# Local attention on one core: two of sixteen query/key projections of a repeat take another place in the written order

## The reference, cut to what matters

```python
def attn_layer(x, Wqkv, qs, ksc, Wo):          # 16 heads of 64
    q, k, v = split(x @ Wqkv, 3)
    q, k = l2norm(q) * qs, l2norm(k) * ksc
    q = q * cos * scale + rotate_half(q) * sin * scale
    k = k * cos / scale + rotate_half(k) * sin / scale
    out = local_attention(q, k, v)             # windows of 32: own window and the one before, softmax
    return out @ Wo
for i in range(6):
    x = attn_layer(shift_tokens(x), ...) + x
    x = ffn_layer(shift_tokens(x), ...) + x    # layer norm, gated GELU
```

## Time and profile before

| | |
|---|---|
| median of 3 runs | 4428.97 us (4423.1 to 4429.79) |
| profiled execution | 4426.65 us |
| its span, first to last instruction | 4424.9 us |
| mean granted TensorE clock | 0.991 of full speed |
| PE busy | 4276.1 us, 97% |
| DVE, ACT, POOL busy | 74%, 59%, 49% |
| matmul instructions, weight loads | 68360 each |

### The profile page before, as it was taken

The page is one execution under the profiler, slowest core; times in us unless marked ns, Lnnn a source line. Parts: engine busy times, 40 slices in busy tenths (PEclk is TensorE's granted clock), DMA queues, the critical chain, the costliest instruction groups (busy, mean ns, idle before and its releaser), DMA issues.

```text
span 4424.9 us, 159360 instructions
## 1 busy us (share of the span) xinstructions
PE 4276.1 (97%) x68360; PEld 2558.4 (58%) x68360; DVE 3267.2 (74%) x5759; ACT 2617.6 (59%) x5346; POOL 2168.4 (49%) x1986
## 2 busy tenths in 40 slices
PE   8999999999799999999999999999999999999998
PEld 5555555555356656656666656656656656656655
DVE  5666666565577878877887877877877777877875
ACT  5544555455356666666666666666666666666664
POOL 0000000000266766766766766766766766766763
PEclk9999999999899999999999999999999999999998
DMA  1000000000111112111121111211122111221112
GB/s 45 4 8 6 8 6 6 6 8 4 46 47 50 48 46 68 50 50 49 49 69 52 48 46 50 69 49 50 48 60 58 44 51 46 62 60 49 49 47 67
DMA packets 141403, 185.95 MB, mean 42 GB/s; under 512 B 32870, under 2 KB 63652, under 8 KB 140708
## 3 DMA queue, kind: packets, MB, share of 16 engines
q1 hardware_dynamic: 140708, 175.76, 14.6%
HBM read 26.76 MB, written 4.19 MB: 7 GB/s over the span
## 4 chain that ended last, share of the span: by engine, by line
PE 70%; issue 1%; DVE 1%; POOL 1%; DMA 0%; SPq 0%; ACT 0%; DVEq 0%; POOLq 0%; ACTq 0%
PE psum L1599 23%; PE psum L1540 10%; PE psum L1604 8%; PE psum L1616 8%; PE psum L1525 6%; PE psum L1637 6%; PE psum L1609 4%; PE psum L1642 3%; PE psum L1562 1%; PE psum L1622 1%; PE psum L1632 0%; POOL qk L1489 0%; POOL cs L1480 0%; DVE cs L1779 0%; DVE rots L1743 0%
## 5 line engine op out<-in xcount | busy, mean ns | idle before, releaser
L1480 POOL TENSOR_TENSOR cs<-cs 128x512 f32<-128x512 f32 x768 | 975.6, 1276 | 545.2 <-DVE cs L1779 526.6
L1599 PE MATMUL psum<-wqkv,xw 128*128 128x512 f32 x2304 | 1184.1, 613 | 10.1 <-DMA wqkv<-in_wqkv 10.1
L1779 DVE TENSOR_TENSOR cs<-psum,rots 128x1024 f32<-128x1024 f32 x768 | 935.1, 1218 | 244.8 <-PE psum L1599 237.0
L1489 POOL TENSOR_TENSOR qk<-cs,rn 128x512 f32<-128x512 f32 x768 | 776.4, 1042 | 407.9 <-ACT rn L1663 407.9
L1676 ACT ACTIVATE sq<-psum 128x512 f32<-128x512 f32 x768 | 459.6, 598 | 538.7 <-DVE cs L1779 176.1
L1508 POOL MEMSET tiled<- 128x128 bf16 x1 | 0.2, 204 | 1170.0 <-POOLq L590 1170.0
L1736 DVE TENSOR_REDUCE ss<-sq 128x8 f32<-128x512 f32 x768 | 519.7, 677 | 11.7
L1540 PEld LDWEIGHTS psum<-pT,vw 64*64 64x64 f32 x18432 | 401.0, 135 | 203.4 <-issue 203.1
L1599 PEld LDWEIGHTS psum<-wqkv,xw 128*128 128x128 f32 x2304 | 371.0, 191 | 179.7 <-issue 139.9
L1540 PE MATMUL psum<-pT,vw 64*64 64x32 f32 x18432 | 446.5, 222 | 22.8 <-issue 18.0
L1604 PEld LDWEIGHTS psum<-ident,qk 128*128 128x128 f32 x3072 | 352.6, 141 | 168.9 <-issue 158.6
(11 more groups left out here) (198 smaller groups left out, 6639.0 us busy)
## 6 DMA issues: line engine op xcount, KB each, us to landing
vw<-vl SPq DMA_DIRECT2D x768, 128.0 KB, 2.4
vw<-vl SPq DMA_DIRECT2D x672, 64.0 KB, 2.0
wqkv<-in_wqkv SPq DMA_DIRECT2D x36, 256.0 KB, 4.2
wol<-in_wol SPq DMA_DIRECT2D x6, 512.0 KB, 3.8
xin<-in_x SPq DMA_DIRECT2D x9, 256.0 KB, 2.9
xr<-in_x SPq DMA_DIRECT2D x8, 256.0 KB, 3.0
sums<-sumout SPq DMA_DIRECT2D x8, 256.0 KB, 2.3
cs<-sums SPq DMA_DIRECT2D x8, 256.0 KB, 4.6
```

Of the source, the lines that this page charges most:

```text
L1480: summed_rot.done(nc.gpsimd.tensor_tensor(own, own, halves(cs[:, t % 2, j, 1, :])[:, :, ::-1, :], ALU.add), at)
L1489: rotated.done(nc.gpsimd.tensor_tensor(qk[:, j, :].rearrange("p (h c) -> p h c", c=EL), cs[:, t % 2, j, 0, :].rearrange("p (h c) -> p h c" ...
L1599: last = nc.tensor.matmul(ps[:, :], xw[:, t * P:(t + 1) * P], wqkv[:, col:col + BANK], start=True, stop=True)
L1779: parts.done(V.tensor_tensor(cs[:, t % 2, j, :, :].rearrange("p i (h c) -> p i h c", c=EL), twice, by_head, ALU.mult), at)
```

## The change

Two names move in `BODY`, and nothing else is edited.

```diff
--- before.py
+++ after.py
@@ -252,10 +252,10 @@
 BODY = [step(name) for name in """
     qk.0.0 t.3.0 qk.0.1 t.3.1 t.3.2 t.3.3 qk.0.2 qk.0.3 n.0 y2.0 pt.2.0 qk.1.0 sa.3
     v.0.0 pt.2.1 s.3.0 s.3.1 v.0.1 t.0.0 t.0.1 w.3 t.0.2 qk.1.1 t.0.3 oa.2
-    qk.1.2 o.2.0 o.2.1 qk.1.3 pt.3.0 sa.0 n.1 pt.3.1 v.1.0 s.0.0 s.0.1 qk.2.0
+    qk.1.2 o.2.0 o.2.1 qk.1.3 pt.3.0 sa.0 n.1 pt.3.1 v.1.0 qk.2.0 s.0.0 s.0.1
     v.1.1 t.1.0 w.0 t.1.1 oa.3 t.1.2 qk.2.1 o.3.0 o.3.1 t.1.3 qk.2.2 pt.0.0
     qk.2.3 v.2.0 sa.1 pt.0.1 qk.3.0 s.1.0 s.1.1 n.2 w.1 y v.2.1 t.2.0
-    t.2.1 xt oa.0 t.2.2 t.2.3 o.0.0 o.0.1 qk.3.1 pt.1.0 pt.1.1 xn qk.3.2
+    t.2.1 xt oa.0 t.2.2 qk.3.1 t.2.3 o.0.0 o.0.1 pt.1.0 pt.1.1 xn qk.3.2
     qk.3.3 sa.2 v.3.0 v.3.1 s.2.0 s.2.1 n.3 gate.0 gate.1 w.2 up.0 gate.2 oa.1
     up.1 up.2 o.1.0 o.1.1
 """.split()]
```

## The result

The changed kernel takes 4454.76 us (median of four runs, 4452.6 to 4457.89); the kernel before takes 4426.03 on the same chip. The ratio is 1.0065, with a 95% interval of 1.0049 to 1.0081: slower by 28.7 us, 22 to 36 by the interval. The profiled executions have spans of 4450.8 and 4424.9, 25.9 us apart; the granted clock is 0.99 in both. Forecast were 16 us more, between 4425 and 4460. Two later executions, one of b_only and one of v_swap, ran at a granted clock of 0.75 and 0.66 and are left out of every comparison.

The account below looks back on a forecast made before the run. The prediction took PE's order to bound the kernel, with pauses for its own instructions. Gains of 28.5 us against costs of 44.6 gave 16.1 more: 4428.97 + 16 = 4445 us, 4436 to 4457 by the terms (8 in 10: 4425 to 4460).

Parts of the forecast that it names:

- oa.3: First move: this step waits for DVE's first centring, behind the product of `qk.2.0`; 0.50 us a repeat, 23.0 us cost.
- sa.2: Second move: this step waits for ACT's copy of `pt.1.0`, last of four behind a square; 15.6 us cost.
- sa.0: First move: new wait for `o.2.0`'s copy, tie lost by 0.03 us, 0.10 for a further waiting instruction; 6.0 us cost.
- o.0.0: Tile 0's first PV half: a projection between the halves takes away 15.2 of 16.7 us of instruction pauses.
- o.3.0: Tile 3's first PV half: PE arrives 0.5 us later where the packet was late; 6.5 of 7.5 us back.
- s.0.0: Tile 0's first score half: a projection between the halves takes away the whole 4.3 us of pauses.
- Waits that don't bind: First rival: pauses go, and bank or copy is free in time at `oa.3` and `sa.2`; 4406 us, chance 0.07.
- Pauses that stay whatever the spacing: Second rival: the pauses stay in number and length, so nothing is given back; 4471 us, chance 0.08.
- Only one large wait binding: Third rival: one of the waits at `oa.3` and `sa.2` doesn't bind, likely `sa.2`; 4429 us, chance 0.13.

Follow-up runs that it names:

- b_only: Kernel before with the second move alone (`qk.3.1` between tile 0's PV halves): ratio 1.0001 to the kernel before.
- v_swap: Kernel before with `v.1.1`, instead of `qk.2.0`, put between the halves of tile 0's scores: ratio 1.0055, 24 us slower.
- b_act_old: Kernel before with the second move (`qk.3.1` between tile 0's PV halves) on PE, ACT's order as before: 4403.44 us, ratio 0.9944.
- sa0_wait: Kernel before, order unchanged, with only the wait for the copy of `o.2.0` added at `sa.0`: ratio 1.0031, 14 us slower.
- a_act_o2: Kernel before with the first move alone (`qk.2.0` between tile 0's score halves), ACT copying `o.2.0` ahead of `qk.1.2`'s square: ratio 1.0036.
- both_act: Changed kernel, but ACT keeps the old order at the second move and copies `o.2.0` ahead of `qk.1.2`'s square: ratio 0.9990 to the kernel before.
- a_only: Kernel before with the first move alone (`qk.2.0` between the halves of tile 0's scores): 4457.09 us, ratio 1.0068.
- shift64: Kernel before with 64 more instructions ahead of PE's first step and no step moved: ratio 1.0014, 6 us slower.
- v01_early: Kernel before with only ACT's copy of `v.0.1` put ahead of the exponentials of `s.3.0` and `s.3.1`: ratio 0.9979, 9 us faster.

## Why the prediction was right, and where it was off

- **`oa.3`: right.** 0.50 us a repeat forecast; the gap grew by 0.46 on average (0.51 in the median repeat). The chain was read correctly from DVE's rows; v_swap shows that two thirds of it is the product in front of the centring. Only the label was forecast wrong: "issue", not L1749.
- **`sa.2`: mechanism right, the number partly luck.** b_act_old shows the cause: with ACT's order of before nothing is held. 15.6 forecast; the wait measured 19.1, and the 15.1 of the table are that less the 4.0 which `sa.2`'s own windows lost, a gain of the move that the prediction didn't have.
- **`sa.0`: mechanism right, size off.** 6.0 forecast, 8.2 measured; bounds 1 to 9. The tie is lost by 0.03 us as forecast (sa0_wait); the waiting instruction behind the release, put at 0.10, is some 0.15.
- **`o.0.0`: right.** 15.2 forecast, 14.4 measured. The spacing works here because the packet keeps its start: `oa.0` isn't newly held, and the packets start at 1.10 before and 1.12 after.
- **`o.3.0`: the step that failed.** "Where the instruction packet was late for `o.3.0`, PE now arrives 0.5 us later", so 6.5 back. The packet arrives 0.5 later too: it starts about 1.1 us *after* the held step does (1.09 and 1.12), wherever that step stands. 2.1 came back, and with the first move alone 0.3.
- **`s.0.0`: also short,** 1.9 of 4.3. The 0.86 us between the halves is there, but the new hold at `sa.0` made the packets 0.77 later. With that hold gone (a_act_o2, both_act) 3.0 and 3.5 came.
- **The sum.** 16.1 forecast. These two terms are 6.8 too high; the rest (`sa.0` 2.2, `s.2.0` 1.4, less 1.7 at `oa.3`, and small ones) brings it to 25.6 of the 25.9 in the span. I had used the packet's start as a fixed time in the earlier trace rows; there the packet of 3219.42 also starts after the first half does, and that could have told.
- **The rivals.** Waits that don't bind: out at all three places. Pauses that stay whatever the spacing: out for `o.0.0`, near the truth for `o.3.0`. Only one large wait binding: out, both do; a_only and b_only give 30 and 0.
- **The total.** 28.7 us by the medians, 1.8 times the 16 forecast, and inside the range of 4436 to 4457: the three costs and `o.0.0` carry it, and the errors in the gains of the first move go one way.

The Trainium skill, "Runtime: NRT & Kernel Launch", section "Instruction fetch mechanics", has the refill in 16 KiB blocks of 256 instructions, which shift64 and the 16.4 KB packets agree with, and calls its cost "mostly hidden". Here `o.2.0`'s pauses alone were 4.6 us of 4425 and `o.0.0`'s 16.7, and v01_early and b_act_old got 4.4 and 14.6 of them back.

**What stays open.** Why `sa.2`'s own windows lose 4 us with the second move, and why `o.0.0` gained 3.9 in v_swap. How far ahead PE's queue works, and at which instruction it asks for a packet, wasn't settled. That the queue's lead is what a hold takes away is the reading that fits sa0_wait, a_act_o2, v01_early and `sa.1` in v_swap; no record shows the queue itself.

## What to carry to other kernels

Where a step that fills in is moved forward on the busiest engine, keep the other engines' order unless they must change: here one square on ACT, moved along for no need, ate a gain of 24 us whole. When an engine waits for its own instructions, look for the last held wait ahead of the packet's start and end that wait sooner; a projection put in between works only if it adds no new hold, since here a hold of under 0.1 us made the packet 0.7 us late. Holding the first of two dense halves doesn't absorb a pause in the second: the packet moved with the half. And where an engine waits for several things, let the one that ends last be waited for last: the other order cost 0.15 us a time here.

## What I had not expected of the hardware

- A packet with PE's instructions starts 1.07 us after the start of a held half and 0.14 us after that of one whose waits are over early, the same list behind both (before and v01_early).
- A pause of a dense half can come from a wait that holds the engine by 0.07 us a repeat (sa0_wait: 3.4 us at the wait, 4.8 in `s.0.0`).
- Which repeats pause follows the count of instructions: 64 more at the head of the list moved the end of every whole episode by three repeats of 2540 instructions, and changed `o.0.0`'s sum by 1.2 us.
- A wait that never holds the engine still moves the packet: ended 0.33 us later, 0.87 us ahead of need, it put it 0.27 us later (`sa.1` in v_swap).
- The same three semaphores cost 0.26 or 0.10 us from the last release to the first matmul, by their order in the waiting instructions (changed kernel and sa0_wait).
